# An attention and FFN layer on one core: TensorE's work regrouped by pairs of tiles, exp moved to the copy out of PSUM, row sums from a ones column

## What is computed

```python
q = (layernorm(x) @ w_q.T + b_q).reshape(B, T, 16, 16)     # B = 8, T = S = 512
k, v = (ctx @ w_k.T + b_k), (ctx @ w_v.T + b_v)            # in the same shape
scores = einsum('bthd,bshd->bhts', q * 0.25, k) + attn_bias
scores = where(key_padding_mask, -3.4e38, scores)
x = x + einsum('bhts,bshd->bthd', softmax(scores), v).reshape(B, T, 256) @ w_out.T + b_out
xn = layernorm(x)
h = silu(fp4(xn) @ fp4(w_gate).T) * (fp4(xn) @ fp4(w_up).T)   # 704 wide
out = x + fp4(h) @ fp4(w_down).T
```

## Time and profile before

| | us |
|---|---|
| median of 3 runs | 1028.66 (1028.31 to 1029.89) |
| the profiled execution, its device time | 1029.46 |
| its span, first to last instruction | 1027.5 |
| first score matmul | 42.6 |
| end of attention's last values matmul | 748.3 |

### The profile page before, as it was taken

One profiled execution on the slowest core, in us unless ns is written; L12 is line 12 of the kernel. 1 busy time (PEld: TensorE's weight loads), 2 busy tenths in 40 slices (PEclk: granted clock), 3 DMA queues, 4 the chain that ended last, 5 costly groups with the idle time before them and its releaser, 6 DMA issues.

```text
span 1027.5 us, 23032 instructions
## 1 busy us (share of the span) xinstructions
PE 952.6 (93%) x6612; PEld 667.7 (65%) x6612; DVE 857.5 (83%) x2125; ACT 722.0 (70%) x1685; POOL 198.6 (19%) x156
## 2 busy tenths in 40 slices
PE   5299999999999999999999999978778999999997
PEld 3176666666657666665765766645456878878885
DVE  3287988888888888888888878899757999999996
ACT  2298988877888888888788888856634555555542
POOL 3222232140240213114024121245400000000000
PEclk9699999999999999999999999999979999999999
DMA  9553451451533335055153433611000000000000
GB/s 290 134 124 76 113 124 27 121 138 28 120 101 90 84 103 123 15 129 132 36 115 93 103 75 89 145 35 31 2 0 6 17 16 15 21 16 15 20 16 26
DMA packets 47339, 76.14 MB, mean 74 GB/s; under 512 B 10016, under 2 KB 26784, under 8 KB 47264
## 3 DMA queue, kind: packets, MB, share of 16 engines
q1 hardware_dynamic: 47264, 75.34, 29.3%
HBM read 20.78 MB, written 4.19 MB: 24 GB/s over the span
## 4 chain that ended last, share of the span: by engine, by line
PE 82%; DVE 8%; issue 5%; SPq 2%; ACT 2%; DMA 1%; DVEq 1%; POOL 0%; ACTq 0%; POOLq 0%
PE psum L967 24%; PE psum L1099 14%; PE psum L1056 12%; PE psum L1235 9%; PE psum L1217 4%; PE psum L1219 4%; PE psum L1218 4%; PE psum L988 3%; PE psum L995 3%; PE psum L1013 2%; PE psum L982 2%; DVE att L845 2%; DVE att L764 2%; SPq L367 1%; SPq L378 1%
## 5 line engine op out<-in xcount | busy, mean ns | idle before, releaser
L569 ACT ACTIVATE att<-att,neg_max 128x512 f32<-128x512 f32 x512 | 367.3, 719 | 119.1 <-DVE neg_max L845 111.9
L845 DVE CUSTOM_DVE_ANT_0 att<-psum,att 128x512 f32<-128x512 f32 x512 | 346.7, 686 | 106.2 <-PE psum L1099 94.2
L967 PE MATMUL psum<-ident,att 128*128 128x128 f32 x2448 | 364.7, 275 | 19.9 <-DVE att L764 7.4
L967 PEld LDWEIGHTS psum<-ident,att 128*128 128x128 f32 x2448 | 298.0, 141 | 94.6 <-issue 45.6
L1099 PE MATMUL psum<-stack 128*128 128x512 f32 x512 | 273.1, 535 | 26.4 <-DMA stack<-kl 17.3
L1099 PEld LDWEIGHTS psum<-stack 128*128 128x128 f32 x512 | 96.7, 189 | 141.4 <-DVE neg_max L845 81.3
L764 DVE COPY att<-psum 128x512 f32<-128x512 f32 x256 | 175.6, 686 | 3.7 <-PE psum L967 3.7
L1056 PE MATMUL psum<-att 128*32 128x256 f32 x2048 | 164.0, 393 | 2.0 <-issue 2.0
L608 ACT ACTIVATE att<-psum 128x512 f32<-128x512 f32 x256 | 150.5, 588 | 18.1 <-PE psum L967 13.1
L1235 PE MATMUL psum<-att 128*128 128x256 f32 (+1 forms) x384 | 98.0, 388 | 2.8 <-ACT att L649 2.8
L569 ACT ACTIVATION_READ_ACCUMULATOR att<-att,neg_max 128x1 f32 x512 | 96.9, 189 | 0.0
(11 more groups left out here) (96 smaller groups left out, 1043.7 us busy)
## 6 DMA issues: line engine op xcount, KB each, us to landing
stack<-qh SPq DMA_DIRECT2D x128, 128.0 KB, 2.4
stack<-ql SPq DMA_DIRECT2D x128, 128.0 KB, 2.3
att<-in_fside_1xSxS_dram SPq DMA_DIRECT2D x16, 512.0 KB, 3.7
stack<-kh SPq DMA_DIRECT2D x128, 64.0 KB, 2.0
stack<-kl SPq DMA_DIRECT2D x128, 64.0 KB, 2.0
att<-in_ctx_dram SPq DMA_DIRECT2D x8, 512.0 KB, 4.8
out_dram<-att SPq DMA_DIRECT2D x32, 128.0 KB, 1.7
x<-in_x_dram SPq DMA_DIRECT2D x1, 3584.0 KB, 20.4
```

The costliest lines, as they stand in the source:

```text
L569: act.activation(prob[:, slot, :], prob[:, slot, :], ACT.Exp, bias=neg_max[:, slot:slot + 1], scale=-1.0, accum_out=row_sum[:, o, tt * 8 + ...
L845: dve.tensor_tensor_reduce(out=prob[:, slot, :], in0=ps_score[:, bank_of(j)[0], :], in1=bias_m[:, tt, :], scale=-1.0, scalar=BIG, op0=ALU. ...
L967: return pe.transpose(out_, in_, ident[:, :])
```

## The change

The attention is written anew around steps of two tiles; the FFN's arithmetic and its row loop stay.

- A step holds one row block of two heads of a pair. PE's order in a step: four transposes of the first tile and four of the second (of the step four before), a piece of a projection, both score matmuls, one group of values (of the step eight before), a second piece in a few steps, and in some steps four small transposes.
- The scores use 48 rows for each head: high by high, low by high and high by low, 16 dimensions each. The first head's lie on partitions 0 to 47, the second's on 64 to 111, each with its own matmul and bank.
- SP writes the high and low parts to an HBM buffer (`planes`), three copies each for q and k, and reads them back into the stack with eight transfers: 14 for an octet.
- The maximum is subtracted in SBUF, by POOL for five of eight tiles and by ACT for three; ACT then takes exp as it copies the transposed tile out of PSUM, for all tiles. There are two banks for transposes, one for each tile of a step; three banks for scores stay, two serve projections and small transposes.
- V has a column of ones after each head (`VW = 17`), so each head's row sum comes out of `values` as row 16 of its 32. The result of four heads is copied (`take_O`), transposed (`make_ot`), divided (`normalise`), and each octet is transposed back (`make_oT`).
- The loop over batches covers 1 to 5, and batches 6 and 7 are unrolled. `prob` has 16 slots instead of 8. The FFN's weights are taken in another order (down first), with their own places in the last batch, and `w_gu_low` has a buffer of its own.

The core of the diff:

```diff
+    STEPS = 16
+    TILES = 2 * STEPS
+    T_LAG = 4
+    V_LAG = 8
+    RING = 16
+    VW = D + 1
...
+        q_hl = sb("q_hl", [P, 2, S], F32R)
+        k_hl = sb("k_hl", [P, 2, S], F32R)
+        qh, ql, kh, kl = q_hl[:, 0, :], q_hl[:, 1, :], k_hl[:, 0, :], k_hl[:, 1, :]
+        stack = sb("stack", [P, 4, 2, 2, S], F32R)
+        q_stack, k_stack = stack[:, :, :, 0, :], stack[:, :, :, 1, :]
...
-        ps_score, ps_T, ps_O, ps_misc = psum[:, 0:3, :], psum[:, 3:6, :], psum[:, 6, :], psum[:, 7, :]
-        PV_AT = (0, 2, 4, 5)
-        T_LAG = 6
-        TAKE_LAG = 6
+        ps_score, ps_O = psum[:, 0:3, :], psum[:, 6, :]
+        ps_T = (psum[:, 3, :], psum[:, 7, :])
+        M0, M1 = psum[:, 4, :], psum[:, 5, :]
...
-            with eng.Fori(1, B - 1) as b:
+            with eng.Fori(1, B - 2) as b:
                 body(b)
+            body(B - 2)
             body(B - 1)
...
+        def exists(n):
+            return not isinstance(n, int) or 0 <= n < N_OCT
+        def parts(s):
+            return s // 8, s % 2, (s % 8) // 2
...
+        def by_act(s, r):
+            return r == 1 and s % 4 != 0
...
+        SCORE_BANK = [j % 3 for j in range(2 * TILES - 1)] + [1]
+        def back_of(j):
+            return next(d for d in range(1, 8) if SCORE_BANK[(j - d) % (2 * TILES)] == SCORE_BANK[j])
...
+        WEIGHTS_AT = {10: (0, M0), 13: (1, M1), 16: (2, M1), 21: (3, M0), 23: (4, M0), 25: (5, M0), 27: (6, M0), 28: (7, M1), 31: (8, M1)}
...
+            def planes_of(m, qk, high_low, ready, done, split):
+                for part in range(2):
+                    wait(sp, ready[part], m + 1)
+                    plain(sp)
+                    for i in split[part]:
+                        sp.dma_start(planes[:, qk, i], high_low[:, part, :].bitcast(F32)).then_inc(done, 16)
...
+            def stack_octet(m, o):
+                wait(sp, q_plane, 48 * (m + 1))
...
-            stack_q(1, 0, 0)
-            stack_k(1, 0)
+                wait(sp, k_plane, 48 * (m + 1))
+                plain(sp)
+                heads = planes.rearrange("(x r) k i d s -> r k (i d) x s", r=2)
+                for h in range(2):
+                    wait(sp, score_ready, TILES * (m - 2) + STEPS * (h + 1))
+                    plain(sp)
+                    slot = 2 * o + h
+                    for r in range(2):
+                        for qk in range(2):
+                            sp.dma_start(stack[64 * r:64 * r + 48, slot, :, qk, :].bitcast(F32),
+                                         heads[r, qk, :, 2 * h:2 * h + 2]).then_inc(stacked[slot], 16)
...
+            def less_max(n, s, r):
+                slot = (2 * s + r) % RING
+                pool.wait_ge(biased, TILES * n + 2 * s + r + 1)
+                pool.tensor_tensor(prob[:, slot, :], prob[:, slot, :], neg_max[:, slot:slot + 1].to_broadcast([P, S]),
+                                   ALU.subtract).then_inc(less_pool, 1)
...
+            def exp_tile(n, s, r):
+                u, (h, kk, tt) = s // 4, parts(s)
+                act.wait_ge(T_ready, TILES * n + 2 * s + r + 1)
+                wait(act, pv_ready, 4 * n + u - 1)
+                act.activation(probT[:, u % 2, 2 * kk + r, :, (tt % 2) * P:(tt % 2 + 1) * P], ps_T[r].rearrange("p (c t) -> p c t", c=SC),
+                               ACT.Exp, scale=1.0 if by_act(s, r) else -1.0).then_inc(exp_ready, 1)
+            def less_max(n, s, r):
+                slot = (2 * s + r) % RING
+                act.wait_ge(biased, TILES * n + 2 * s + r + 1)
+                act.activation(prob[:, slot, :], prob[:, slot, :], ACT.Identity, bias=neg_max[:, slot:slot + 1],
+                               scale=-1.0).then_inc(less_act, 1)
...
+            def step(b, S_):
+                first, last = is_first(b), is_last(b)
+                drain = isinstance(b, int) and b == B
+                if S_ % 8 == 0:
+                    n, o, s = place(b, S_ - 16)
+                    if exists(n):
+                        take_O(n, s // 8)
+                n, o, s = place(b, S_ - T_LAG)
+                late = exists(n)
+                if late:
+                    exp_tile(n, s, 0)
...
+                m, o, s1 = place(b, S_ - 1)
+                if exists(m) and by_act(s1, 1):
+                    less_max(m, s1, 1)
+                if late:
+                    exp_tile(n, s, 1)
             def body(b):
-                period(b, 0)
...
+            def normalise(m, o, h, src):
...
+                dve.wait_ge(ot_ready, quad + 1)
+                v = src.rearrange("p (t j m) -> p t j m", t=NT, j=4)
+                dve.reciprocal(inv_sum[:, :, :], v[:, :, :, D]).then_inc(inv_ready, 1)
+                dve.wait_ge(inv_ready, quad + 1)
+                col = o * P + h * 4 * D
+                dve.tensor_tensor(O_n[:, :, col:col + 4 * D].rearrange("p t (j d) -> p t j d", d=D), v[:, :, :, 0:D],
+                                  inv_sum[:, :, :].unsqueeze(3).to_broadcast([P, NT, 4, D]), ALU.mult).then_inc(ot_taken, 1)
...
+            def less_scores(b, S_, r):
+                n, o, s = place(b, S_)
+                h, kk, tt = parts(s)
+                t = TILES * n + 2 * s + r
+                slot = (2 * s + r) % RING
+                dve.wait_ge(score_ready, t + 1)
+                if o == 0 and s < 8:
+                    dve.wait_ge(bias_ready, 4 * b + tt + 1)
+                wait(dve, T_ready, t - RING + 1)
+                plain(dve)
+                dve.tensor_tensor_reduce(out=prob[:, slot, :], in0=ps_score[:, SCORE_BANK[2 * S_ + r], :], in1=bias_m[:, tt, :], scale=-1.0,
+                                         scalar=BIG, op0=ALU.add, op1=ALU.min,
+                                         accum_out=neg_max[:, slot:slot + 1]).then_inc(biased, 1)
...
+            def make_ot(quad, bank):
+                pe.wait_ge(O_taken, quad + 1)
                 for tt in range(NT):
-                    last = transposes(ps_misc[:, tt * P:(tt + 1) * P], inv_exp[:, tt].rearrange("p h d -> p (h d)"))
-                last.then_inc(r_ready, 1)
...
+            def make_oT(m, o, bank):
+                pe.wait_ge(ot_taken, 2 * m + 2)
+                for tt in range(NT):
+                    last = transposes(bank[:, tt * P:(tt + 1) * P], O_n[:, tt, o * P:(o + 1) * P])
+                last.then_inc(oT_ready, 1)
...
+            def scores(b, S_):
+                n, o, s = place(b, S_)
+                h, kk, tt = parts(s)
+                if s % 8 == 0:
+                    pe.wait_ge(stacked[2 * o + h], 64 * (b + 1))
+                for r in range(2):
+                    j = 2 * S_ + r
+                    wait(pe, biased, b * 2 * TILES + j - back_of(j) + 1)
+                for r in range(2):
+                    rows = slice(64 * r, 64 * r + 48)
+                    pe.matmul(ps_score[:, SCORE_BANK[2 * S_ + r], :], q_stack[rows, 2 * o + h, kk, tt * P:(tt + 1) * P],
+                              k_stack[rows, 2 * o + h, kk, :], start=True, stop=True).then_inc(score_ready, 1)
+            def transpose_tile(b, S_, r):
+                n, o, s = place(b, S_ - T_LAG)
+                if not exists(n):
                     return
-                pe.wait_ge(exp_ready, i + 1)
-                bank, back = bank_of(j)
-                e = j - back
-                wait(pe, T_even if e % 2 == 0 else T_odd, (i - back) // 2 + 1 if isinstance(i, int) else place["period"] * (TILES // 2) + e // 2 + 1)
+                t = TILES * n + 2 * s + r
+                wait(pe, exp_ready, t - 1)
+                pe.wait_ge(less_act if by_act(s, r) else less_pool, taken_off(n, s, r))
                 for c in range(SC):
-                    last = transposes(ps_T[:, bank, c * P:(c + 1) * P], prob[:, j % RING, c * P:(c + 1) * P])
+                    last = transposes(ps_T[r][:, c * P:(c + 1) * P], prob[:, (2 * s + r) % RING, c * P:(c + 1) * P])
                 last.then_inc(T_ready, 1)
-            place = {}
-            def values(o, u, c, units):
-                half, r = u // 2, u % 2
+            def values(b, S_):
+                n, o, s = place(b, S_ - V_LAG)
+                if not exists(n):
+                    return
...
+                for j in range(4):
+                    col = (4 * h + j) * VW
+                    last = pe.matmul(ps_O[32 * j:32 * j + 32, half * 2 * P:(half + 1) * 2 * P], vv[:, o, c, col:col + 2 * D],
+                                     probT[:, u % 2, j, c, :], start=c == 0, stop=c == SC - 1)
                 if c == SC - 1:
                     last.then_inc(pv_ready, 1)
...
+                place_batch["b"] = b
+                for S_ in range(2 * STEPS):
+                    transpose_tile(b, S_, 0)
+                    transpose_tile(b, S_, 1)
+                    heavy(b, S_, 0)
+                    scores(b, S_)
+                    values(b, S_)
+                    heavy(b, S_, 1)
+                    light(b, S_)
```

(3 more changed lines are left out.)

1072 lines of the change are left out of this document (552 added, 520 removed).

## The result

The changed kernel takes 1056.3 us (median of 4 runs, 1054.8 to 1057.2); the kernel before, beside it, 1029.3. The ratio is 1.026, interval 1.024 to 1.028. I had forecast 1015, range 976 to 1048: wrong in sign, and outside the range. The profiled execution is 1054.8, span 1052.7, so 25.2 over the span of before.

A forecast was written before the change was run, and what follows sets the result against it. PE was taken to bound middle batches, DVE the last. 1029.5 less 9 (start), less 1 (first batch), plus 12.6 (middle batches), less 2.2 (jump), less 14 (last batch, tail) is 1015.9; less 0.8 for the median, 1015; range 976 to 1048.

The forecast's parts named there:

- DVE's 93.6 falls by 19 to 75: Last batch: DVE's busy time drops from 93.6 us to 75 as it loses its copies.
- the price of the jump: Border between batches: the loop's jump costs PE about 2.2 us; one jump fewer gives -2.2.
- "hidden" for SP's later order: SP after the start: 14 transfers per octet instead of 32, with the next half stacks' reads adding no time.
- the gain of 9 at the start: Start: fewer SP transfers but an added HBM round trip bring the first score 9 us earlier; bounds 4 and 14.
- rival B: Scores: the two row halves run one after the other, +38 us, 1053; chance 0.12.
- The third form: Scores in row halves: a third form of TensorE's array, its change priced at 0.165 us a step; bounds nothing and 0.165.
- rival A: Scores: the third array form costs nothing, -37 us with 5 given back by ACT's chain, 983; chance 0.18.
- The 0.06 for a second weight load: Score pair on PE: 0.06 us added to 0.23 for loading the second matmul's weights.
- POOL takes the bound: Last batch: POOL, busy 90 us, sets the time; last transposes wait for it until about 91 us after the start.
- rival D: Last batch: POOL loses more than thought, the gain falls to 5 us, 1024; chance 0.07.
- New tail +2: After the last values: copy, transposes, normalise and transposes back cost 2 us more.
- Rival C: PE waits on ACT's exp for a transpose bank: 5 us a batch, forecast under 0.7; total 1046; chance 0.16.

The follow-up runs named there:

- act_last: The changed kernel with every subtraction of the maximum in the last batch's two octets given to ACT, none to POOL: 1044.3 us.
- ctx_first: The changed kernel with the next context's load issued, in batch 0 alone, ahead of octet 1's key planes and stack reads on SP: 1049.3 us.
- exp_first: The changed kernel with context load first, batches 1 to 5 unrolled, last-batch subtraction on ACT, x load split, and second tile's exp right behind the first's: 1001.6 us.
- unroll_dve: The changed kernel with the loop over batches unrolled on DVE alone, the other engines still jumping: 1034.0 us.
- exp_first_paired: The kernel of exp_first with two steps' values groups issued together after the odd step's scores: 990.9 us, ratio 0.962 to the kernel before.
- full_form: The changed kernel with both score matmuls over all 128 partitions instead of 48 rows each, for timing only: 1061.3 us.
- tile1_late: The changed kernel with the second tile's transposes put behind the scores and ahead of the values: 1071.6 us.

## Why the prediction was wrong, step by step

The steps that failed are, by size, the last batch's "DVE's 93.6 falls by 19 to 75" (12.0, by act_last, of the 17.8 missing there), the price of the jump (9, of which better steps cover 5), "hidden" for SP's later order (7.0, by ctx_first, of the 11.6 missing in batch 0), and the gain of 9 at the start (5.5 short).

**What was right.** The scores run side by side (3 ns apart): rival B is out, and the rule I had cited from the Trainium skill, TensorE: Matmul & The Clock Gate, Part 3, about 4 ns between concurrent row tiles, agrees. The third form is paid: I took 0.165, and the runs give 0.145 for one more change, 0.18 for the row halves as a whole; rival A is out. The 0.06 for a second weight load was not there. PE's middle batch without the jump is 84.7 where I had 85.7 (85.2 and 0.5), though with 0.9 and not 0.5 of waits on ACT in it. ACT's 57 and DVE's 53 in a middle batch are 57.5 and 50 to 55; POOL's 67 is 54 to 58, as a subtraction takes 1.065, the lower of my bounds, not 1.28.

**The jump.** "One jump fewer -2.2" and six batches with a border of 2.2 took the price of the old border for the new. It is 2.0 in the old kernel, 5.0 in the new: the four jumps cost 19.8 where the forecast's five had 11, 9 us too little, and half of that is hidden in the table by the steady steps, 5 better than forecast. DVE's jump had been read as DVE's idle time and PE's share of it; that another body pays another price I hadn't considered, nor that the clock falls behind it. Why the price differs is not known.

**Batch 0.** "Later SP and POOL order: hidden" weighed the stack reads, the planes and the bias, and not the context's load, which the same queue now issues behind them: the step left out an instruction that was moved past. 7.0 by ctx_first. Another 2.2 is exp's order; with both gone batch 0 is 77.1, near the 76.8 of before the change.

**Start.** Gain 3.5 instead of 9. Planes landed at 32.3, not at 28 to 29, and reads take 6.7 from the first issue, not 2. I had the row for a slow early transfer (5.4 us) and took the later one.

**Last batch and tail.** "DVE's 93.6 falls by 19 to 75" failed: it was 88.1, since an operation's duration was taken as its own when POOL's busy time beside it was to double (42.5 to 83.3). With the subtractions off POOL it is 74.8. "POOL takes the bound" failed with it: PE waits 5.2 for POOL and 8.2 for DVE, so neither is the bound alone. This is near rival D, that POOL loses more than I thought, at 12.0 by act_last where D had 9. In exp_first, which has all four edits, the stretch is 86.0 + 294.3 = 380.3, 13.0 under before. That it is near the 14 I had forecast is in part luck: its end has the clock at the lower level for 10.2 us, that of before for 17.0. New tail +2 was too little: in unroll_dve, with 17.0 too, the end is 297.2 for 292.5, so 4.7; what is left of the 298.4 goes with the clock (23.8).

**Rival C** looked excluded by the profile's list of waits, which has 0.3 us of PE waiting for exp in batch 6, under the 0.7 of my own sign. Its mechanism was there: 0.9 a middle batch, 10.3 in all, though not the 34 of its price. In this profile a wait between two matmuls of one group doesn't stand as idle time; it makes the group longer (1.05 for 0.93).

With the measured parts the sum is 1029.5 - 3.5 + 10.6 + 14.3 + 3.8 = 1054.7, for a profiled 1054.8.

## What to carry to other kernels

When work moves to an idle engine, ask which other engine's operations run beside it, and price those again: a duration from the trace holds only with the neighbours it had. List every transfer that a queue issues, not only the new ones, and find for each who waits for it. Before reordering a tuned matmul stream, put the consumer that frees its banks first; only then does a saved change of the array's form show (here 0.15 us each, 10.7 us in the kernel; with the old order of exp the same edit made it 14.1 slower). And give the old kernel what you give the new one: without its jumps it is 11.4 faster.

## What the runs showed of the hardware

- A jump back on DVE leaves it idle 4.4 to 5.4 us in this kernel, 5.2 with two batches in the body; from the branch to the next instruction it is 4.7 to 5.7 us, against 2.8 to 3.0 in the kernel before and 0.1 to 0.3 on ACT, POOL and SP. The Trainium skill, Advanced Engine Details and Errata, section "Control Flow Timing", has about 108 ns for a compare-and-branch; the branch's own record is 0.06 us here, but what DVE loses by it is the 5 us behind it, and for that the measurement decides.
- Leaving TensorE's row halves costs about 0.21 us, to the column groups (scores to values 0.43 less a pass of 0.213) and to the full array alike (580.09 to 580.52 is 0.43 too); entering them from the full array 0.09 (last projection to score 0.31 for 0.22: 579.78 to 580.09 in exp_first_paired). Only the sum of about 0.3 is firm: where the scores too take the full array (full_form), the first of them starts 0.03 after the last projection's start, so a record's start doesn't tell how the price is shared. What full_form and tile1_late give by whole steps, 0.18 and 0.145, needs no such reading.
- At each of the four borders with a jump, where PE had waited 2.0 to 3.0 us, the granted clock then fell to the lower of its two levels (0.50 over 218.5 to 221.9, 1.2 GHz; 1.00 over the 77 us from 223), so the wait costs more than its own length: PE waited 2.75 at a border that cost 5. At the borders of the kernel before, with no wait of PE over 1.04, it stayed at the higher level (1.00 over 50 to 746).
- With POOL's subtraction beside it a DVE scalar operation of 0.43 us took 1.15, and a reduction of 0.68 kept its time.
